# The joint round of a decoder kernel: the turn of the averaged scores goes behind the whole network product, the turn of the attention's norm into its middle

## The chip, the cores and the metric

The kernel runs on one core of a Trainium2 chip. The metric is the device time of one execution in microseconds (us). TensorE (PE) multiplies matrices and turns (transposes) tiles, VectorE (DVE), ScalarE (ACT) and GpSimd (POOL) work on elements, and SyncE (SP) starts transfers. Each engine works through its own instructions in their written order; semaphores tie the orders together.

## What is computed

The reference is a decoder of two layers over x of 16 batches x 256 rows x 256 columns, in float32. The first layer is a windowed attention, a cross attention over 77 context rows, and a network with 8 experts of which each row takes one. The second layer, which holds the change, is cut here to its core:

```python
# L1_attn: a state over the 16 batches (RWKV), then channel mixing
xx = ln(x); k, v, r = mixes of xx and of the batch before, times Wk, Wv, Wr
x = x + (sigmoid(r) * wkv(k, v)) @ Wo.T
yy = ln(x); x = x + sigmoid(rr) * (square(relu(kk)) @ Wcv.T)
# L1_xattn: attention over the context, averaged over 4 heads, steers a state space model
scores = Q @ K.T / sqrt(32)                  # 4 heads, 77 context rows
topv, topi = top_k(scores, 32); attn = softmax over those 32, zero elsewhere
attn_mean = attn.mean(heads); c_t = attn_mean @ V
scale_in, shift_in, scale_out, shift_out = c_t @ W_film_in, c_t @ W_film_out
x = layernorm(x_text) * (1 + g * scale_in) + g * shift_in
y = s4d(x)                                   # through a Fourier transform
xt = x_text + y * (1 + g * scale_out) + g * shift_out
xt = layernorm(xt + gelu(layernorm(xt) @ W1 + b1) @ W2 + b2)
# L1_ffn: product with the signs of a weight matrix, scale, bias, clip
```

## The kernel before, in words

The first layer takes up to about 815 us. The second layer is one block, `mixing_and_state_space` (from line 1430), with one written program for each engine. Its loop has 20 rounds, `for n in range(B + 4)` with B = 16 batches, and each round works on five batches at once, each at another stage: t = n (state), c = n - 1 (channel mixing, then the norm hE, queries and keys), j = n - 2 (scores, the 32 largest, average, film), i = n - 3 (Fourier transform, spectrum, inverse, network) and p = n - 4 (last norm, signs, output). A stage whose batch isn't in 0 to 15 is left out: rounds 0 to 2 have no network product, round 16 has no state batch and round 17 no hE either.

What sets the order around the change is written by hand in three places. (Line numbers are those of the kernel before.)

- TensorE, lines 2481 to 2551. A round ends with `hidden(i, 1)`, `network(n, i, 0, ...)` and the first half of `network(n, i, 1, ...)` (24 matmuls at L2462), then `turn_average` (L2399; it waits for `am`, turns its two 128x77 tiles into the bank p_T, L2403), the other half of the network product (8 matmuls, L2462), `turn_E` (L2361; turns the norm hE into the same bank p_T, four matmuls at L2287), `film(j, 0)` (L2406; waits for amT, two products of 512 columns in four matmuls at L2413), `queries_keys` (L2366; waits for hT; L2369, L2371, L2372) and `film(j, 1)`, which waits for `hs`, VectorE's use of the first film product. The next round begins with `keys_D` (L2305), `turn_2` and `values_D`.
- ScalarE, lines 2211 to 2278. After the two `gelu` come `h_E(c)` (the norm hE, L2032), `average(j)` (copies the turned average from p_T to amT, L2170), `n_2(t)` (the norm before channel mixing, L2032, which `turn_2` of the next round reads), in rounds 0 and 1 `keep_context` (copies projected context tiles from PSUM to SBUF, L2163), then `turned(e["Th"], e["hT"], c)` (copies turned hE to xT, L2142), `film(j, 0)` (L2175), `queries(c)` (L2147), `h_1(t + 2)` (L2032) and `film(j, 1)`. The next round begins with `fall_4` (L2090), the mixes of channel mixing (L2044) and others.
- VectorE, lines 1960 to 2015. `average(j)` ends with the reduction into `am` (L1867). After it come the statistics of the batch t + 2, `add_mix`, `bounded` (L1940, L1942) and `film(j, 0)` (L1873, L1875, L1877, the last of which gives `hs`). The next round brings, among others, the scores, `add_channel_mix` (L1804, which TensorE's `receptance`, L2293, waits for) and, after the inverse transform, `scale_out` (L1903).

GpSimd makes the factors of all norms (`rstd`, L1599 to L1604). No queue of transfers stands in the changed lines.

The bank p_T is used by both turns, so each must wait until ScalarE has copied what the one before left. The helper `latest(engine, (sem, i), ...)` waits for the first pair of its list whose i is a batch, `past(engine, sem, i)` for batch i of that semaphore if i is not negative:

```python
def latest(engine, *users):
    for sem, i in users:
        if 0 <= i < B:
            engine.wait_ge(sem, i + 1)
            return
```

Of the kernel before, what the change touches and what calls it, by code (L numbers as in the profile page):

```python
# [24 lines left out]
B, S, D = 16, 256, 256  # L25
# [1396 lines left out]
# [8 lines that stand above are left out]
def mixing_and_state_space(nc, args, k, place, ys_dram, cxT, cxU, out, ahead, lw, folded_film, folded_row, spectrum_in):  # L1430

    J, C, H, DH, DM = 77, 192, 4, 32, 4 * D
    FB = DM // P
# [6 lines left out]
    with ExitStack() as ctx:  # L1440
# [577 lines left out]
        def _(act):  # L2018
# [88 lines left out]
            def n_2(t):  # L2107
                act.wait_ge(d["rs2"], t + 1)
                past(act, z["T2"], t - 1)
                apply(L2, x1, n3, d["n2"])  # L2110
# [29 lines left out]
            def turned(sem, to, i):  # L2140
                act.wait_ge(sem, i + 1)
                a_.activation(xT[:], p_T[:], ACT.Copy).then_inc(to, 1)  # L2142
# [23 lines left out]
            def average(j):  # L2166
                act.wait_ge(e["amp"], j + 1)
                if j == 0:
                    act.wait_ge(d["init"], 10)
                a_.activation(amT[0:J, :], p_T[0:J, 0, :], ACT.Copy).then_inc(e["amT"], 1)  # L2170
# [40 lines left out]
            for n in range(B + 4):  # L2211
                t, c, j, i, p = n, n - 1, n - 2, n - 3, n - 4
                if t < B:
                    fall_4(t)
                if 0 <= c < B:
                    channel_mixes_A(c)
                if t < B:
                    values(t)
                    gates(t)
                    falls(t)  # L2220
                if 0 <= c < B:
                    channel_mixes_B(c)
                    gate_channel(c)
                if 0 <= p < B:
                    h_6(p)
                if 0 <= c < B:
                    rectify(c, 0, 0)
                    rectify(c, 0, 1)
                if 0 <= p < B:
                    turned(f["T6"], f["h6T"], p)  # L2230
                if t < B:
                    exps_D(t)
                if t + 1 < B:
                    n_1(t + 1)
                if n == 0:
                    keep_context(2, 3)
                if 0 <= c < B:
                    square(c, 0)
                    rectify(c, 1, 0)
                    rectify(c, 1, 1)  # L2240
                    square(c, 1)
                if t + 1 < B:
                    mixes_A(t + 1)
                    if n == 0:
                        keep_context(4, 5)
                    mixes_B(t + 1)
                if n == 1:
                    keep_context(8)
                if 0 <= i < B:
                    n_3(i)  # L2250
                if 0 <= i < B:
                    turned_3(i)
                if 0 <= j < B:
                    exps_E(j)
                    n_E(j)
                if 0 <= i < B:
                    gelu(i, 0)
                    gelu(i, 1)
                if 0 <= c < B:
                    h_E(c)  # L2260
                if 0 <= j < B:
                    average(j)
                if t < B:
                    n_2(t)
                if n == 0:
                    keep_context(6, 7)
                if n == 1:
                    keep_context(9)
                if 0 <= c < B:
                    turned(e["Th"], e["hT"], c)  # L2270
                if 0 <= j < B:
                    film(j, 0)
                if 0 <= c < B:
                    queries(c)
                if t + 2 < B:
                    h_1(t + 2)
                if 0 <= j < B:
                    film(j, 1)

        @block.tensor  # L2280
        def _(pe):
# [78 lines left out]

            def turn_E(n, j):  # L2361
                pe.wait_ge(e["h"], j + 1)
                latest(pe, (e["amT"], n - 2), (e["n3T"], n - 3), (d["mB"], n + 1))
                turn(hE[:, j % 2]).then_inc(e["Th"], 1)

            def queries_keys(j):  # L2366
                pe.wait_ge(e["hT"], j + 1)
                for kb in range(KD):
                    te.matmul(p_T[:, 0, :], Wq[:, kb, :], xT[:, kb, :], start=kb == 0, stop=kb == KD - 1)  # L2369
                rows = slice(64 * (j % 2), 64 * (j % 2) + 64)  # L2370
                te.matmul(p_T[:, 1, 0:J], Wk[:, 0, :], cxT[:, j % 2, j // 2, :], start=True, stop=False)  # L2371
                te.matmul(p_T[:, 1, 0:J], Wk[rows, 1, :], cxU[rows, j % 2, j // 2, :], start=False, stop=True).then_inc(e["qk"], 1)  # L2372
# [25 lines left out]

            def turn_average(n, j):  # L2399
                pe.wait_ge(e["am"], j + 1)  # L2400
                latest(pe, (e["n3T"], n - 3), (d["mB"], n + 1))
                for t in range(2):
                    last = te.transpose(p_T[0:J, 0, t * P:(t + 1) * P], am[:, t, :], k["ident"][:])  # L2403
                last.then_inc(e["amp"], 1)
# [51 lines left out]
            def network(n, i, a, first, end):  # L2456
                if a == 0:
                    latest(pe, (d["x1"], n), (z["g2"], n - 1), (e["Yr"], n - 3))
                for fb in range(first, end):
                    if a == 0 and fb % 2 == 0:  # L2460
                        pe.wait_ge(e[f"g{fb // 4}{fb // 2 % 2}"], i + 1)
                    last = te.matmul(p_Y[:, a, :], hid[:, fb, a * P:(a + 1) * P], W2[:, fb, :],  # L2462
                                     start=fb == 0, stop=fb == FB - 1)
                if end == FB:
                    last.then_inc(e["ffp"], 1)
# [15 lines left out]
            for n in range(B + 4):  # L2481
                t, c, j, i, p = n, n - 1, n - 2, n - 3, n - 4
                if n == 3:
                    pe.wait_ge(lw["third"], 64)
                    pe.wait_ge(cw["wide"], 16)
                if n == 4:
                    pe.wait_ge(f["sign"], 1)
                if t < B:
                    keys_D(n, t)
                if 0 <= c < B:  # L2490
                    turn_2(n, c)
                if t < B:
                    values_D(n, t)
                if 0 <= j < B:
                    scores(j)
                if t < B:
                    receptance_D(n, t)
                if n == 0:
                    context(2, 3)
                if 0 <= i < B:  # L2500
                    forward(i)
                if 0 <= c < B:
                    receptance(n, c)
                    channel(n, c, 0)
                if 0 <= p < B:
                    turn_6(n, p)
                if 0 <= c < B:
                    channel(n, c, 1)
                if 0 <= i < B:
                    inverse(n, i)  # L2510
                if t + 1 < B:
                    turn_1(n, t + 1)
                if 0 <= p < B:
                    project(n, p)
                if n == 0:
                    context(4, 5)
                if n == 1:
                    context(8)
                if 0 <= c < B:
                    channel_out(n, c, 0, 0, FB)  # L2520
                    channel_out(n, c, 1, 0, FB // 2)
                if 0 <= i < B:
                    turn_3(n, i)
                if 0 <= c < B:
                    channel_out(n, c, 1, FB // 2, FB)
                if 0 <= i < B:
                    hidden(i, 0)
                if n == 0:
                    pe.wait_ge(lw["first"], 16 * 8)
                if t < B:  # L2530
                    out_product(n, t)
                if n == 0:
                    context(6, 7)
                if n == 1:
                    context(9)
                if 0 <= i < B:
                    hidden(i, 1)
                    network(n, i, 0, 0, FB)
                    network(n, i, 1, 0, FB // 2)
                if 0 <= j < B:  # L2540
                    turn_average(n, j)
                if 0 <= i < B:
                    network(n, i, 1, FB // 2, FB)
                if 0 <= c < B:
                    turn_E(n, c)
                if 0 <= j < B:
                    film(j, 0)
                if 0 <= c < B:
                    queries_keys(c)
                if 0 <= j < B:  # L2550
                    film(j, 1)
# [78 lines left out]
```

## Time and profile before

| | us |
|---|---|
| median of 3 runs | 1811.51 |
| lowest and highest | 1810.51, 1813.48 |
| the profiled execution | 1824.46 |
| its span | 1822.8 |
| TensorE busy, share of the span | 1610.8, 88% |
| VectorE busy | 1278.0, 70% |
| ScalarE busy | 909.9, 50% |
| GpSimd busy | 649.1, 36% |

The span is the time from the first to the last instruction of the profiled execution; all rows of the trace are on its clock. Busy time of TensorE is modelled from the starts of its matmuls, which overlap by a little, so two groups one after the other may seem to share a tenth of a microsecond. "Granted clock" is the share of TensorE's full 2.4 GHz that the chip let through: 1.00, or 0.50 for 1.2 GHz. In a row of the trace, "[1.45 <-DVE E_am L1867]" says that the engine stood idle for 1.45 us before it, and that the instruction of that engine and line ended the wait.

### The profile page before, as it was taken

The page shows a single profiled execution, that of the slowest core. Times are in us where ns is not written, and L with a number is a line of the kernel's source. Part 1 is how long each engine was busy: PE and PEld are TensorE (multiplying, and loading weights), DVE is VectorE, ACT ScalarE, POOL GpSimd, SP SyncE. Part 2 cuts the span into 40 slices and gives each one's busy share as a digit, 9 for nine tenths or more (in the row PEclk, how much of TensorE's full clock was granted, in tenths as well). Part 3 has the DMA queues.
Part 4 walks back from the last instruction along what each step waited for, and adds up shares of the span by engine and source line. Part 5 has one row for each costly group of instructions (what it writes and reads, how often), then busy time and mean ns, then how long its engine had stood idle before and what let it go on. Part 6 is the DMA issues. An engine that isn't in the chain of part 4 may idle for free.

```text
span 1822.8 us, 27958 instructions
## 1 busy us (share of the span) xinstructions
PE 1610.8 (88%) x8584; PEld 1330.1 (73%) x8584; DVE 1278.0 (70%) x4255; ACT 909.9 (50%) x1943; POOL 649.1 (36%) x1005
## 2 busy tenths in 40 slices
PE   6899999997599999978869999999999999998774
PEld 3677778776489999874647777777877777786553
DVE  3566777766247666224478899999999999987751
ACT  2454444442142222226656766667776667763221
POOL 1022322222101000015435556666655655552111
PEclk9899999999699999998879999999999999999877
DMA  9992000000796565545200000000000000000000
GB/s 258 289 290 75 15 16 13 12 13 24 256 309 199 153 202 162 174 139 212 73 7 8 13 20 19 20 13 7 20 19 20 20 13 7 8 14 13 7 6 12
DMA packets 145477, 143.47 MB, mean 79 GB/s; under 512 B 22587, under 2 KB 128525, under 8 KB 145074
## 3 DMA queue, kind: packets, MB, share of 16 engines
q1 hardware_dynamic: 128321, 119.78, 21.4%
q10 hardware_dynamic: 13936, 13.50, 2.3%
q0 software_dynamic: 3072, 8.39, 1.5%
q8 instruction: 71, 1.16, 0.3%
q14 instruction: 77, 0.62, 0.1%
HBM read 87.71 MB, written 53.94 MB: 78 GB/s over the span
## 4 chain that ended last, share of the span: by engine, by line
PE 28%; DVE 21%; issue 3%; ACT 2%; POOL 1%; DMA 0%; POOLq 0%; DVEq 0%; ACTq 0%
PE E_pK L2346 6%; PE E_pK L2305 3%; PE E_pS L2413 3%; DVE E_wk L1850 3%; PE E_pY L2462 3%; DVE E_ex L1782 2%; DVE E_m L1843 2%; PE E_pY L2293 2%; PE E_pU L2422 2%; PE E_pY L2431 2%; DVE E_st L1715 1%; PE E_pY L2305 1%; PE E_pT L2287 1%; PE E_pY L2356 1%; PE E_pU L2452 1%
## 5 line engine op out<-in xcount | busy, mean ns | idle before, releaser
L1294 ACT ACTIVATE F_uT<-F_puT,F_b 128x128 f32<-128x128 f32 x312 | 88.4, 371 | 214.6 <-PE F_puT L1351 165.4
L1351 PEld LDWEIGHTS F_puT<-F_hT,F_W 128*128 128x128 f32 x1248 | 157.8, 207 | 10.3 <-DVE F_hT L1089 8.1
L1351 PE MATMUL F_puT<-F_hT,F_W 128*128 128x128 f32 x1248 | 159.6, 291 | 5.7 <-DVE F_hT L1089 5.7
L1599 POOL TENSOR_SCALAR E_var<-E_mv 128x2 f32<-128x2 f32 x80 | 44.6, 558 | 309.8 <-DVE E_mv L1719 308.2
L1364 PE MATMUL F_py<-C_W,F_uT 128*128 x624 | 141.2, 379 | 0.6 <-DVE C_shared L1101 0.6
L2452 PE MATMUL E_pU<-E_xT,E_W 128*128 128x256 f32 x512 | 122.5, 395 | 5.3 <-ACT E_hid L2193 3.1
L1364 PEld LDWEIGHTS F_py<-C_W,F_uT 128*128 128x128 f32 x624 | 115.5, 190 | 15.1 <-issue 1.0
L2356 PE MATMUL E_pY<-E_Wcv,E_hid 128*128 128x256 f32 x512 | 118.3, 385 | 8.6 <-issue 8.2
L2462 PE MATMUL E_pY<-E_W,E_hid 128*128 128x256 f32 x512 | 119.1, 387 | 0.1
L2452 PEld LDWEIGHTS E_pU<-E_xT,E_W 128*128 128x128 f32 x512 | 101.6, 199 | 21.7 <-ACT E_hid L2193 3.9
L2346 PE MATMUL E_pK<-E_cmix,E_Wck 128*128 128x256 f32 x512 | 115.9, 381 | 0.0
L2356 PEld LDWEIGHTS E_pY<-E_Wcv,E_hid 128*128 128x128 f32 x512 | 96.1, 192 | 26.5 <-issue 14.3
L1066 POOL TENSOR_SCALAR F_var<-F_mv 128x1 f32<-128x1 f32 x39 | 8.6, 222 | 290.8 <-DVE F_mv L1078 290.8
L2462 PEld LDWEIGHTS E_pY<-E_W,E_hid 128*128 128x128 f32 x512 | 98.1, 194 | 14.0 <-DVE E_x L1796 0.9
L2346 PEld LDWEIGHTS E_pK<-E_cmix,E_Wck 128*128 128x128 f32 x512 | 96.8, 191 | 12.9
L237 POOL TENSOR_SCALAR A_varB<-A_mvB 128x2 f32<-128x2 f32 x16 | 3.5, 220 | 256.2 <-DVE A_mvB L289 256.2
L1850 DVE MATCH_REPLACE8 E_wk<-E_m,E_wk 128x77 f32<-128x77 f32 x384 | 80.4, 222 | 0.0
L2193 ACT ACTIVATE E_hid<-E_pU,b 128x256 f32<-128x256 f32 x128 | 52.1, 473 | 51.2 <-PE E_pU L2452 51.0
L645 PE MATMUL A_pqa<-A_hTB,A_Wq 128*128 128x256 f32 x256 | 68.1, 413 | 2.6 <-ACT A_hTB L490 2.6
L2305 PE MATMUL E_pK<-E_mix,Wkvr 128*128 128x256 f32 x256 | 64.6, 398 | 5.0 <-DVE E_mix L1752 5.0
L1602 POOL TENSOR_TENSOR E_rs<-E_var,minus_half 128x2 f32<-128x2 f32 x80 | 62.5, 782 | 6.7
L2305 PEld LDWEIGHTS E_pK<-E_mix,Wkvr 128*128 128x128 f32 x256 | 49.9, 201 | 18.3 <-issue 12.1
(432 smaller groups left out, 4133.4 us busy)
## 6 DMA issues: line engine op xcount, KB each, us to landing
F_W<-in_L_ffn_W SPq DMA_DIRECT2D x39, 1024.0 KB, 6.0
sorted_x<-zero SPq DMA_DIRECT2D x8, 4096.0 KB, 31.6
C_W<-in_L_ffn_W ACTq DMA_DIRECT2D x8, 1024.0 KB, 7.6
F_xs<-sorted_x SPq DMA_DIRECT2D x39, 128.0 KB, 2.7
F_b<-in_L_ffn_b SPq DMA_DIRECT2D x39, 128.0 KB, 3.2
sorted_y<-C_shared ACTq DMA_DIRECT2D x39, 128.0 KB, 2.9
context_film<-E_W SPq DMA_DIRECT2D x8, 512.0 KB
out<-E_tB SPq DMA_DIRECT2D x16, 256.0 KB, 2.2
```

Of the source, the lines that this page charges most:

```text
L645: last = te.matmul(p_qa[:, half, (m % 2) * S:(m % 2 + 1) * S], Wq[:, kb, m * P:(m + 1) * P], hTB[:, kb, :], start=kb == 0, stop=kb == KD - 1)
L1294: last = nc.scalar.activation(uT[:, i % 2, f, :], p_uT[:, i % 2, half, (f % 4) * P:(f % 4 + 1) * P], ACT.Gelu, bias=b1[:, i % 2, f:f + 1])
L1351: last = nc.tensor.matmul(p_uT[:, i % 2, half, (f % 4) * P:(f % 4 + 1) * P], W1[:, i % WB, kb, f * P:(f + 1) * P], hT[:, i % 2, kb, :], st ...
L1364: last = nc.tensor.matmul(p_y[:, 0:D], uT[:, i % 2, f, :], W2[:, bass.ds(e, 1), f, :], start=f == 0, stop=f == FB - 1)
L1602: chained(g.tensor_tensor(L["rs"][:], L["var"][:], k["minus_half"][:], ALU.pow))
L1850: last = v.match_replace(wk[:, t, hd, :], m8[:, turn, t, hd, :], src[:, t, hd, :], TAKEN)
L2305: last = te.matmul(to[:, o, :], Wkvr[:, m, kb, o * P:(o + 1) * P], mix[:, m, kb, :], start=kb == 0, stop=kb == KD - 1)
L2346: last = te.matmul(p_K[:, q, :], Wck[:, kb, fb * P:(fb + 1) * P], cmix[:, 0, kb, :], start=kb == 0, stop=kb == KD - 1)
L2356: last = te.matmul(p_Y[:, a, :], hid[:, fb, a * P:(a + 1) * P], Wcv[:, fb, :], start=fb == 0, stop=fb == FB - 1)
L2413: last = te.matmul(p_S[:, q, :], amT[:, t * P:(t + 1) * P], VW[j % 2][:, q * 512:(q + 1) * 512], start=True, stop=True)
L2452: last = te.matmul(p_U[:, q, :], W1[:, kb, fb * P:(fb + 1) * P], xT[:, kb, :], start=kb == 0, stop=kb == KD - 1)
L2462: last = te.matmul(p_Y[:, a, :], hid[:, fb, a * P:(a + 1) * P], W2[:, fb, :], start=fb == 0, stop=fb == FB - 1)
```

## The change

In TensorE's order the turn of hE comes right after the first half of `network(n, i, 1, ...)`, then the other half, then the turn of the averaged scores. ScalarE's order follows: the copy of turned hE comes before the copy of the average, and `n_2` comes behind both, in rounds 0 and 1 also behind `keep_context(6, 7)` and `keep_context(9)`. The waits for the bank p_T are rewritten to fit: `turn_E` no longer waits for amT of its round, `turn_average` waits for hT, and `queries_keys` waits for amT.

```diff
@@ -2258,16 +2258,16 @@
                 if 0 <= c < B:
                     h_E(c)
-                if 0 <= j < B:
-                    average(j)
-                if t < B:
-                    n_2(t)
                 if n == 0:
                     keep_context(6, 7)
                 if n == 1:
                     keep_context(9)
                 if 0 <= c < B:
                     turned(e["Th"], e["hT"], c)
+                if 0 <= j < B:
+                    average(j)
+                if t < B:
+                    n_2(t)
                 if 0 <= j < B:
                     film(j, 0)
@@ -2360,11 +2360,12 @@
             def turn_E(n, j):
                 pe.wait_ge(e["h"], j + 1)
-                latest(pe, (e["amT"], n - 2), (e["n3T"], n - 3), (d["mB"], n + 1))
+                latest(pe, (e["n3T"], n - 3), (d["mB"], n + 1))
                 turn(hE[:, j % 2]).then_inc(e["Th"], 1)
 
             def queries_keys(j):
                 pe.wait_ge(e["hT"], j + 1)
+                past(pe, e["amT"], j - 1)
@@ -2398,7 +2399,7 @@
             def turn_average(n, j):
                 pe.wait_ge(e["am"], j + 1)
-                latest(pe, (e["n3T"], n - 3), (d["mB"], n + 1))
+                latest(pe, (e["hT"], n - 1), (e["n3T"], n - 3), (d["mB"], n + 1))
@@ -2537,12 +2538,12 @@
                     hidden(i, 1)
                     network(n, i, 0, 0, FB)
                     network(n, i, 1, 0, FB // 2)
+                if 0 <= c < B:
+                    turn_E(n, c)
+                if 0 <= i < B:
+                    network(n, i, 1, FB // 2, FB)
                 if 0 <= j < B:
                     turn_average(n, j)
-                if 0 <= i < B:
-                    network(n, i, 1, FB // 2, FB)
-                if 0 <= c < B:
-                    turn_E(n, c)
                 if 0 <= j < B:
                     film(j, 0)
```

## Rows read from the trace of the kernel before

**Rows 1.** The page: busy us, share of the span, instructions.

```profile
PE 1610.8 (88%) x8584; PEld 1330.1 (73%) x8584; DVE 1278.0 (70%) x4255; ACT 909.9 (50%) x1943; POOL 649.1 (36%) x1005
```

**Rows 2.** Stretches: length, busy of PE, PEld, DVE, ACT, POOL, granted clock, DMA.

```profile
899.50:903.00 3.50, 3.42 (x9) 2.79 (x10) 0.00 (x0) 0.36 (x2) 2.70 (x7) 0.50 0.44 122
...
1354.00:1407.00 53.00, 50.05 (x231) 41.35 (x230) 48.97 (x166) 37.33 (x79) 33.25 (x46) 1.00 0.05 17
```

**Rows 3.** The chain in order of time, round 10: start, us, what.

```profile
1379.09 1.20 DVE E_am L1867
...
1407.25 0.70 DVE E_fo L1903
...
1432.71 1.20 DVE E_am L1867
```

**Rows 4.** Timeline of TensorE, end of round 10: start, us, what, idle before.

```profile
1373.55 5.34 PE L2462 MATMUL E_pY<-E_W,E_hid 128*128 128x256 f32 x24
1380.34 0.44 PE L2403 MATMUL E_pT<-ident,E_am 128*77 128x128 f32 x2 [1.45 <-DVE E_am L1867]
1380.62 1.89 PE L2462 MATMUL E_pY<-E_W,E_hid 128*128 128x256 f32 x8
1382.35 0.60 PE L2287 MATMUL E_pT<-ident,E_hE 128*128 128x128 f32 x4
1382.79 1.88 PE L2413 MATMUL E_pS<-E_VW,E_amT 78*128 78x512 f32 x4
...
1386.04 1.98 PE L2413 MATMUL E_pS<-E_VW,E_amT 78*128 78x512 f32 x4
```

**Rows 5.** Timeline of ScalarE, the same place.

```profile
1380.82 0.38 ACT L2170 ACTIVATE E_amT<-E_pT 77x256 f32<-77x256 f32 x1 [5.26 <-PE E_pT L2403]
```

**Rows 6.** Timeline of VectorE, the same place.

```profile
1383.24 0.69 DVE L1942 TENSOR_TENSOR E_tB<-E_tB,E_X 128x512 f32<-128x512 f32 x1
1384.78 0.42 DVE L1873 TENSOR_TENSOR E_u<-E_u,E_pS 128x256 f32<-128x256 f32 x1 [0.84 <-PE E_pS L2413]
...
1385.57 0.41 DVE L1877 TENSOR_TENSOR E_hE<-E_hE,E_pS 128x256 f32<-128x256 f32 x1
```

**Rows 7.** Timeline of TensorE, rounds 2, 3 and 16.

```profile
949.00 1.08 PE L2287 MATMUL E_pT<-ident,E_hE 128*128 128x128 f32 x4 [0.56 <-ACT E_amT L2170]
...
1003.41 0.61 PE L2403 MATMUL E_pT<-ident,E_am 128*77 128x128 f32 x2 [2.68 <-DVE E_am L1867]
...
1007.54 1.88 PE L2413 MATMUL E_pS<-E_Wvf,E_amT 78*128 78x512 f32 x4
...
1702.98 0.38 PE L2403 MATMUL E_pT<-ident,E_am 128*77 128x128 f32 x2
```

**Rows 8.** Timelines of all engines, end of round 1 and start of round 2.

```profile
892.79 1.11 PE L2395 MATMUL E_pU<-E_Wvf,cxU 64*104 64x512 f32 x4
...
897.04 1.09 ACT L2032 ACTIVATE E_n<-E_x,E_nmr,E_rs 128x256 f32<-128x256 f32 x2 [3.40 <-POOL E_nmr L1604]
898.04 1.00 ACT L2163 ACTIVATE E_W<-E_pU 104x1024 f32<-104x1024 f32 x1
...
898.94 0.58 ACT L2142 ACTIVATE E_xT<-E_pT 128x512 f32<-128x512 f32 x1
...
899.58 2.08 PE L2369 MATMUL E_pT<-E_xT,E_Wq 128*128 128x256 f32 x4 [5.09 <-ACT E_xT L2142]
899.70 0.20 POOL L1604 TENSOR_TENSOR E_nmr<-E_nm,E_rs 128x2 f32<-128x2 f32 x1
...
907.10 0.91 ACT L2090 ACTIVATE E_ex<-E_diff,E_decay 128x256 f32<-128x256 f32 x2 [3.01 <-DVE E_diff L1758]
907.91 1.91 ACT L2044 ACTIVATE E_cmix<-E_pT,E_biasA,E_scaleA 128x256 f32<-128x256 f32 x4
...
911.34 1.22 DVE L1804 TENSOR_TENSOR E_cmix<-E_cmix,E_cmixB 128x1024 f32<-128x1024 f32 x1
...
912.91 1.96 PE L2293 MATMUL E_pY<-E_Wcr,E_cmix 128*128 128x256 f32 x8 [0.78 <-ACT E_gate_ L2084]
```

## The prediction, made before the change was run

> **What bounds the kernel now.** I read the page first, then the chain of waits of the last stage, then each engine's timeline for one round, then the rounds at both ends. TensorE is busy 88% and VectorE 70% of the span [rows 1]: neither alone is full. From about 893 us on, 20 rounds n = 0 to 19 run; a regular one takes 53.62 us (the chain's two reductions into `am`, 1379.09 and 1432.71 [rows 3]). The reader should see a loop of two engines there. From 1380.34 to 1407.25 the chain is all TensorE, ending in the inverse transform; from 1407.25 to the end of the reduction into `am` at 1433.9 it is all VectorE [rows 3], with no gap that another engine ends. The two meet at the turn of the averaged scores: TensorE stands 1.45 us there for `am` and only then does half a network product (1.73 us, 1380.62 to 1382.35) and the turn of hE (0.44), neither of which needs `am`; then the film product starts at 1382.79 [rows 4]. So 1.73 + 0.44 us of free work stand behind the wait. That is what the change moves.
>
> **Part 1: regular rounds, n = 4 to 14, eleven of them.** TensorE ends the first part of the network product at 1378.89 (1373.55 + 5.34), the next could start 0.16 earlier, as matmuls overlap by that much (1380.62 + 1.89 against 1382.35) [rows 4]. In the new order: turn of hE 1378.73 to 1379.17, second half to 1380.90, then the turn of the scores. `am` is there at 1380.29 (1379.09 + 1.20 [rows 3]), so TensorE no longer waits and VectorE has some 0.6 us in hand. The price is new: the copy of the turned scores to amT, hidden before by the half product, is now bare between turn and film. The turn takes 0.38 when nothing held it (row 1702.98 [rows 7]) and the copy 0.38 [rows 5]. The wait around that same copy is seen in round 2, 0.56 us at half clock (row 949.00 [rows 7]); it can't be under 0.38; I take 0.47, as the hand-overs there are partly slowed by the low clock. Film then starts at 1380.90 + 0.38 + 0.47 = 1381.75, 1.04 earlier than 1382.79. It is now started by a wait: its loads are not ahead, and the second film product, started like that, lasts 1.98 against 1.88 [rows 4], so 0.94 is left at its end. VectorE ends its own work at 1383.93 [rows 6], so its film step can begin at about 1383.87 instead of 1384.78, 0.91 earlier; the second film product starts 0.06 after that step's last instruction ends (1385.98 and 1386.04 [rows 4, 6]), so it is bound by it. I take **0.90 a round, 9.9 for eleven**; ends 0.4 (a second wait eats half) and 1.04.
> The ScalarE moves cost nothing here: the copy of turned hE runs at 1379.4 to 1380.0, beside the half product (it is 0.6 long by the equal copy in row 898.94 [rows 8]); the channel mixing's norm (n_2) slips behind amT, but its own turn on TensorE comes only behind film, queries, the second film product and the keys. Without that cover n_2 would hold film's ScalarE copy by its 1.09. The turn of hE needs ScalarE's norm of it, which stands ahead of all the moved work in ScalarE's order and is done while TensorE is in the first part of the network product. `queries_keys` gains a wait for an older amT, long fulfilled since film has waited for the newer one. No DMA moves; SP and POOL are passed by nothing.
>
> **Part 2: rounds 3 and 15.** Here the wait for `am` is 2.68 us, and the half product after it ran at half clock: 4.13 us from turn to film (1003.41 to 1007.54) where a regular round has 2.45 [rows 4, 7]. Moved ahead, 2.17 us of work fill the wait to 0.5, and film starts 0.44 + 0.47 after the turn: 4.13 - 0.91 = **3.2 each, 6.4**; round 15 repeats the pattern. Low end 2.5 each.
>
> **Part 3: round 2.** There is no network; the turn of hE stood between amT and film (949.00, 0.88 long up to film [rows 7]). It now runs in the idle time before. Gain 0.9 if the clock rises as much earlier, 0.46 if it rises at the same moment; **0.7**.
>
> **Part 4: rounds 16 and 17.** TensorE comes late and does not wait (row 1702.98 has no idle time [rows 7]). Nothing is filled, and the bare copy is paid, with the film's 0.10 and overlap: about 0.65 each, **-1.3**; ends -0.9 and -1.5.
>
> **Part 5: the start, rounds 0 and 1, where ScalarE's order matters.** In round 1 ScalarE stood until 897.04 for the factor of n_2, and behind n_2 were the copy of a context tile (1.00) and of turned hE (0.58), so the query product began only at 899.58, after 5.09 us of idle, at a granted clock of 0.50, 1.2 GHz [rows 2, 8]. In the new order these two run first: the context product ends at 893.90 (892.79 + 1.11), the copies at 893.94 to 895.45, queries from 895.5, 4.1 us earlier. The idle time before is then 1.0, less than the 1.45 that leaves the clock at 1.00 [rows 2, 4], so I expect queries and keys at 2.4 GHz, half as long. The next bound is then POOL: it ends the norm of the next batch at 899.90 (row 899.70 [rows 8]), ScalarE applies it (1.09) and begins the falls at 901.05 instead of 907.10; 0.81 + 1.81 of ScalarE and 1.22 of VectorE later, with hand-overs, 905.05, the receptance product starts, against 912.91 [rows 8]: **7.9**. Low end 4.0, if the clock falls all the same. In round 0 n_2 goes behind two context copies, the second of which can't start until its product ends: a loss between nothing and its own 1.09 [rows 8]; **-0.35**, since most of the wait for that product is used by the first copy.
>
> **Sum.** 9.9 + 6.4 + 0.7 - 1.3 + 7.9 - 0.35 = 23.2 us. The profiled execution took 1824.46 (span 1822.8), so 1801.2 (span 1799.6); the runs' median 1811.51 is 12.95 below it, and the same 23.2 comes off: **1788.3**. By the ends of all parts: gains of 0.4 x 11 + 5.0 + 0.46 - 1.5 + 4.0 - 1.09 = 11.3 to 1.04 x 11 + 6.4 + 0.9 - 0.9 + 7.9 = 25.7, so 1785.8 to 1800.2.
>
> **The clock, and a rule against the change.** Each regular round has a few idle spots on TensorE, the longest of 1.45 us, and its granted clock stays 1.00 [rows 2, 4]; the change replaces the longest by one of 0.47. The Trainium skill, in "TensorE: Matmul & The Clock Gate", section "HAM oscillation", warns that frequent small idle spots between groups of matmuls can make the clock fall again and again. By that rule a new spot before film in every round could cost; by this trace it would not, and the sum keeps to the trace.
>
> **Rivals.**
> 1. *Round 1 gives only its earlier start* (the clock falls anyway, or another wait follows): 4.0 for 7.9, total 19.3, 1792.2. For it: a long quiet stretch stands around it. Chance 0.15.
> 2. *A second wait in regular rounds*: the film step of VectorE comes 0.1 to 0.5 later than I have it, or `am` comes after TensorE again. Gain 0.4 a round: total 17.7, 1793.8. For it: VectorE's 0.84 of idle before film shrinks to nothing [rows 6], so both engines are now tight. Chance 0.17.
> 3. *The loop is VectorE's alone*, so regular rounds gain nothing: 13.3, 1798.2. Against: the chain runs 26.9 us on TensorE in each round [rows 3]. It is also what we should see if the moved order changed nothing there. Chance 0.05.
> 4. *Slower: the bare wait drops the clock at film.* If film and queries ran at 1.2 GHz in rounds 3 to 16, film would be 1.7 longer (it doubles) and the query product 1.0 (half of round 1's 2.08 at a clock of 0.50 [rows 2, 8]): 2.7 x 14 = 38 on top of 1788.3, so 1826. It decides from 1.65 us a round on. Against it: the longer spots of now leave the clock at 1.00. Chance 0.03.
> The forecast has 0.57; another mix of parts that ends within 0.2% of before 0.03.
>
> **How the numbers follow.** 0.2% (3.6 us) is about what a measurement of this kernel can tell from no change. The forecast and rivals 1 to 3 are all faster by more: 0.94; same 0.03; slower 0.03. The range takes the forecast's ends and rivals 1, 2 and 3, with 1 to 1.5 us on either side for the spread of the runs shown (1810.51 to 1813.48): 1784 to 1801.
>
> **What would show it.** Right: regular rounds of 52.7 us; at the turn of the scores no idle time on TensorE and then 0.4 to 0.6 "<-ACT E_amT" before film; the wait of 2.68 gone and the network product in rounds 3 and 15 at full clock; queries of round 1 at 895.5 and at 2.4 GHz, the receptance product of round 2 near 905; in rounds 16 and 17 film 0.6 later after the network. Wrong: a turn that still waits for `am`, a query product at half clock in round 1, or TensorE waiting for VectorE's film step for more than 0.2.

## The result, and the profile after

In the same series the changed kernel takes 1792.47 us in the median of four runs (1791.12 to 1799.51), the kernel before 1812.49 (four runs, 1810.51 to 1817.97): a ratio of 0.9884, 95% interval 0.9845 to 0.9923. Two later series with the same code gave 0.9859 (0.983 to 0.9889) and 0.9869 (0.9827 to 0.9911). The forecast of 1788.3 against 1811.51 is a ratio of 0.9872. So the kernel is faster, by about as much as was said: 20.0, 22.9 and 21.0 us between medians, where 23.2 had been summed. The measured 1792.47 lies inside the stated range of 1784 to 1801.

The profiled execution after has a span of 1797.8, 25.0 less than before. Not all of this is the change. The rounds begin at another moment in every execution: `add_mix` of round 0 (L1752), which the change leaves alone, starts at 859.17 before and at 856.32 after, and between 842.5 and 859.2 in all profiles of this study. So below, next to medians, stands **the rest**: the span less the start of that instruction. It is 963.63 before and 941.48 after, 22.15 less, and tells a few microseconds apart where medians can't.

The page after, busy time of each engine (answers to [rows 1]; the work is the same, so TensorE's share is higher by the time it no longer stands):

```profile
PE 1606.7 (89%) x8584; PEld 1323.5 (74%) x8584; DVE 1278.7 (71%) x4255; ACT 909.8 (51%) x1943; POOL 651.2 (36%) x1005
```

Stretches after: the query and key products of round 1, the film, query and key products of round 2, and one regular round (columns as in [rows 2]):

```profile
892.80:896.30 3.50, 3.46 (x17) 2.94 (x18) 0.61 (x3) 1.42 (x3) 3.10 (x7) 1.00 0.44 122
936.90:950.50 13.60, 13.56 (x26) 7.94 (x27) 5.79 (x12) 3.16 (x7) 5.95 (x10) 0.51 0.15 42
1327.00:1380.00 53.00, 51.03 (x237) 42.30 (x236) 49.60 (x167) 38.23 (x80) 33.31 (x46) 1.00 0.05 17
```

A regular round is at a granted clock of 1.00 as before, and so are now the products of round 1 [rows 2 had 0.50]. Those of round 2 are at half clock.

The chain of waits after, up to the turn of the scores and film of round 11, a regular round like the round 10 of [rows 3] (all rows of 1396 to 1422 below are of round 11):

```profile
1396.66 0.98 ACT E_n L2032 x2
...
1408.71 5.18 PE E_pY L2463 x24
1413.89 0.44 PE E_pT L2287 x4
1414.33 1.73 PE E_pY L2463 x8
1416.06 0.23 PE E_pT L2404 x2
...
1416.31 0.39 ACT E_amT L2170
...
1416.74 1.98 PE E_pS L2414 x4
```

VectorE's 26.7 us from the inverse transform to `am`, which stood in the chain before, are gone from it: the chain now reaches film through TensorE and, earlier in the round, ScalarE. The same place of round 11 in TensorE's timeline (to be read beside [rows 4]):

```profile
1408.55 5.34 PE L2463 MATMUL E_pY<-E_W,E_hid 128*128 128x256 f32 x24
1413.73 0.60 PE L2287 MATMUL E_pT<-ident,E_hE 128*128 128x128 f32 x4
1414.16 1.89 PE L2463 MATMUL E_pY<-E_W,E_hid 128*128 128x256 f32 x8
1415.89 0.38 PE L2404 MATMUL E_pT<-ident,E_am 128*77 128x128 f32 x2
1416.74 1.98 PE L2414 MATMUL E_pS<-E_Wvf,E_amT 78*128 78x512 f32 x4 [0.47 <-ACT E_amT L2170]
...
1420.14 1.98 PE L2414 MATMUL E_pS<-E_Wvf,E_amT 78*128 78x512 f32 x4
```

ScalarE there (answers to [rows 5]):

```profile
1416.31 0.38 ACT L2170 ACTIVATE E_amT<-E_pT 77x256 f32<-77x256 f32 x1 [1.35 <-PE E_pT L2404]
```

VectorE there (answers to [rows 6]):

```profile
1414.12 1.20 DVE L1867 TENSOR_REDUCE E_am<-E_ex 128x154 f32<-128x616 f32 x1
...
1418.27 0.69 DVE L1942 TENSOR_TENSOR E_tB<-E_tB,E_X 128x512 f32<-128x512 f32 x1
1418.88 0.41 DVE L1873 TENSOR_TENSOR E_u<-E_u,E_pS 128x256 f32<-128x256 f32 x1
...
1419.67 0.41 DVE L1877 TENSOR_TENSOR E_hE<-E_hE,E_pS 128x256 f32<-128x256 f32 x1
```

Read the three together. The turn of the scores has no idle time before it: `am` ended at 1415.32 (1414.12 + 1.20), 0.57 earlier. Film waits 0.47 for ScalarE's copy, no more. VectorE's first film instruction follows L1942 without a gap, where 0.84 stood before, and its last ends at 1420.08, 0.06 before the second film product. Every one of these was forecast, and successive turns of the scores lie 52.70 apart (52.7 forecast).

TensorE in rounds 2, 3 and 16 (answers to [rows 7]):

```profile
926.96 1.11 PE L2287 MATMUL E_pT<-ident,E_hE 128*128 128x128 f32 x4 [2.56 <-ACT E_hE L2032]
935.76 0.71 PE L2404 MATMUL E_pT<-ident,E_am 128*77 128x128 f32 x2 [7.69 <-DVE E_am L1867]
936.94 3.78 PE L2414 MATMUL E_pS<-E_VW,E_amT 78*128 78x512 f32 x4 [0.47 <-ACT E_amT L2170]
...
943.34 3.78 PE L2414 MATMUL E_pS<-E_VW,E_amT 78*128 78x512 f32 x4
946.91 3.58 PE L2305 MATMUL E_pK<-E_mix,Wkvr 128*128 128x256 f32 x8
...
994.23 0.44 PE L2404 MATMUL E_pT<-ident,E_am 128*77 128x128 f32 x2 [0.51 <-DVE E_am L1867]
995.14 1.98 PE L2414 MATMUL E_pS<-E_Wvf,E_amT 78*128 78x512 f32 x4 [0.47 <-ACT E_amT L2170]
...
1679.73 0.38 PE L2404 MATMUL E_pT<-ident,E_am 128*77 128x128 f32 x2
1680.59 1.98 PE L2414 MATMUL E_pS<-E_VW,E_amT 78*128 78x512 f32 x4 [0.47 <-ACT E_amT L2170]
```

Round 3's wait is 0.51 for 2.68, round 16 pays the bare copy, and in round 2 both film products and the keys run at half clock.

All engines, end of round 1 and start of round 2 (answers to [rows 8]):

```profile
891.28 1.02 ACT L2163 ACTIVATE E_W<-E_pU 104x1024 f32<-104x1024 f32 x1 [0.30 <-PE E_pU L2396]
892.20 0.59 ACT L2142 ACTIVATE E_xT<-E_pT 128x512 f32<-128x512 f32 x1
892.85 1.13 PE L2370 MATMUL E_pT<-E_xT,E_Wq 128*128 128x256 f32 x4 [1.02 <-ACT E_xT L2142]
...
897.50 1.09 ACT L2032 ACTIVATE E_hD<-E_X,E_nmr,E_rs 128x256 f32<-128x256 f32 x2 [1.69 <-POOL E_nmr L1604]
898.50 0.89 ACT L2090 ACTIVATE E_ex<-E_diff,E_decay 128x256 f32<-128x256 f32 x2
...
901.30 1.22 DVE L1804 TENSOR_TENSOR E_cmix<-E_cmix,E_cmixB 128x1024 f32<-128x1024 f32 x1 [0.41 <-issue]
```

The copies no longer stand behind the norm that waits for POOL; the queries begin after 1.02 of idle instead of 5.09 and take 1.13 instead of 2.08; the next bound is POOL's `nmr`, as forecast.

### The profile page after: what moved, and what is told of

Its sections match the earlier page's. It is cut to its first block, busy times and chain, and to the rows that moved or that the text cites. A ratio compares the mean times of both kernels' runs of the same rounds, so it can differ in the third digit from the quotient of the medians.

```text
span 1797.8 us, 27973 instructions
## 1 busy us (share of the span) xinstructions
PE 1606.7 (89%) x8584; PEld 1323.5 (74%) x8584; DVE 1278.7 (71%) x4255; ACT 909.8 (51%) x1943; POOL 651.2 (36%) x1005
## 4 chain that ended last, share of the span: by engine, by line
PE 34%; ACT 10%; DVE 6%; issue 3%; POOL 1%; DMA 0%; ACTq 0%; POOLq 0%; DVEq 0%
PE E_pU L2453 6%; PE E_pY L2463 5%; PE E_pS L2414 3%; PE E_pK L2346 3%; PE E_pK L2305 3%; PE E_pY L2293 3%; PE E_pY L2356 2%; ACT E_mix L2044 2%; ACT E_mixB L2044 2%; PE E_pU L2423 2%; PE E_pY L2305 1%; PE E_pT L2287 1%; ACT E_ex L2105 1%; ACT E_hid L2119 1%; PE E_pS L2382 1%
## 5 line engine op out<-in xcount | busy, mean ns | idle before, releaser
L1351 PEld LDWEIGHTS F_puT<-F_hT,F_W 128*128 128x128 f32 x1248 | 150.2, 198 | 11.1 <-DVE F_hT L1089 9.0
L1351 PE MATMUL F_puT<-F_hT,F_W 128*128 128x128 f32 x1248 | 152.0, 282 | 6.6 <-DVE F_hT L1089 6.6
L2356 PE MATMUL E_pY<-E_Wcv,E_hid 128*128 128x256 f32 x512 | 116.6, 381 | 8.6 <-issue 8.2
L2356 PEld LDWEIGHTS E_pY<-E_Wcv,E_hid 128*128 128x128 f32 x512 | 94.9, 190 | 26.0 <-issue 14.3
L645 PEld LDWEIGHTS A_pqa<-A_hTB,A_Wq 128*128 128x128 f32 x256 | 53.6, 216 | 14.9 <-ACT A_hTB L490 6.9
```

The lines of the kernel that those rows point to most:

```text
L645: last = te.matmul(p_qa[:, half, (m % 2) * S:(m % 2 + 1) * S], Wq[:, kb, m * P:(m + 1) * P], hTB[:, kb, :], start=kb == 0, stop=kb == KD - 1)
L1351: last = nc.tensor.matmul(p_uT[:, i % 2, half, (f % 4) * P:(f % 4 + 1) * P], W1[:, i % WB, kb, f * P:(f + 1) * P], hT[:, i % 2, kb, :], st ...
```

## The experiments

Each kernel was timed beside the kernel before. "The change" is the changed kernel; times are medians, ratios are against the kernel before. The rest is compared between profiles with the same length of `channel_out` (L2356) in round 2, for a reason told under the fourth experiment.

**The change again.** No edit.

> The changed kernel once more, as the base for the others of this set. The sum of the prediction with the parts as its first profile has them gives 22 us less than before; the runs so far say 20. Theory (all parts real): 20 to 23 less than the kernel before. Rival (part of the 25 us between the two profiles is other work): the profile again shows a time ahead of round 0 that differs by some us from before, which no part of the change touches. In round 2 the granted clock stayed at half until 950 us in the first profile; if that belongs to the change, the film product there again lasts 3.8 and the keys product behind it 3.6.

1790.37, ratio 0.9859 (0.983 to 0.9889); rest 941.69 against 941.48 in the first profile; regular rounds 52.70. The regular part of the trace repeats.

**ScalarE's order at the start, alone.** The kernel before, with only this:

```diff
-                if t < B:
+                if 1 < n < B:
                     n_2(t)
...
                     turned(e["Th"], e["hT"], c)
+                if n < 2:
+                    n_2(t)
```

> The kernel before with ScalarE's new order in rounds 0 and 1 alone: n_2 behind the context copies and behind the copy of turned hE. Theory (part 5 is 7.9 less 0.35, independent of the rest): 7.5 us less than before, about 1805; queries of round 1 start some 4 us earlier and run at 2.4 GHz; regular rounds stay at 53.6. Rival 1 (only the earlier start counts): 4 less. Second rival (the start gains only together with TensorE's order): 0.

1805.66, ratio 0.9954 (0.9929 to 0.998): 7.6 less. The queries of round 1 start after 1.02 of idle and take 1.13, and the receptance product of round 2 starts 46.24 after `add_mix` where it was 53.74 before: 7.5 less, as expected. Regular rounds keep 53.63. The rest, 960.05, is only 3.6 less than before, because the clock stayed low for longer behind the turn of the scores in round 2 (see Part 3 in the last sections). One norm, moved on one engine in two rounds of twenty, carries a third of the gain.

**The change without it.** `n_2` in its old place in rounds 0 and 1, all else as changed.

> The changed kernel with n_2 back in its old place in rounds 0 and 1 alone. Theory: the rest of the change remains, 9.9 + 6.4 - 1.3 and what round 2 gives or takes (+0.7 to -2): 13 to 15.5 us less than before, 7.5 more than the change; regular rounds at 52.7. Rival (the parts share one gain): less than 4 more than the change.

1798.40, ratio 0.991 (0.9879 to 0.9941): 8.0 more than the change; by the rest 948.12 against 941.69, 6.4 more. The query product stands 5.10 idle and is at half clock again. The receptance product of round 2 starts 52.35 after `add_mix`, 6.1 later than in the change and not 7.5, since the clock came back within the key product of round 1 (3.25 long, 3.78 in the profile of before). So the size of Part 5 hangs in part on when the clock comes back. The parts add: 7.6 and 14.9 less, each alone, make 22.5, and the whole change in the same series was 22.9 less.

**The old order in round 2.** The change, but in round 2 TensorE turns hE behind the scores, and ScalarE copies in that order:

```diff
-                if 0 <= c < B:
+                if 0 <= c < B and n != 2:
                     turn_E(n, c)
...
                     turn_average(n, j)
+                if n == 2:
+                    turn_E(n, c)
```

> The changed kernel with the old order in round 2 alone: turn of the scores, its copy, then turn and copy of hE. Theory A (the early turn of hE, standing alone in TensorE's idle time, has to do with the clock coming back late): film and keys of round 2 run at 2.4 GHz sooner, 2 to 3 us less than the change. Theory B (when the clock comes back is chance, not the order): the order costs the turn's own 0.9 at half clock, so 0.5 to 1 more than the change, and the rise of the clock lies anywhere in both.

1793.10, ratio 0.9873 (0.9843 to 0.9904); rest 944.31. TensorE's timeline in its round 2:

```profile
904.98 8.83 PE L2358 MATMUL E_pY<-E_Wcv,E_hid 128*128 128x256 f32 x32 [2.46 <-issue]
...
928.01 0.71 PE L2406 MATMUL E_pT<-ident,E_am 128*77 128x128 f32 x2 [11.35 <-DVE E_am L1867]
929.27 1.09 PE L2289 MATMUL E_pT<-ident,E_hE 128*128 128x128 f32 x4 [0.56 <-ACT E_amT L2170]
930.15 3.62 PE L2416 MATMUL E_pS<-E_VW,E_amT 78*128 78x512 f32 x4
...
936.39 3.78 PE L2416 MATMUL E_pS<-E_VW,E_amT 78*128 78x512 f32 x4
```

Two lines need care. The long channel product takes 8.83 here and 7.14 in the change's first two profiles, after the same 2.46 of idle: in some executions the clock falls there and in some not. The third profile of the change, below, has 8.83, so this is chance and no effect of an order; it is worth 1.7. Like with like (both 8.83), film starts 83.26 after `add_mix` in the old order and 82.31 in the new (929.77 - 847.46): the moved turn is worth 0.95 at that place. And the second film product is 3.78 long here too, in the old order. So the new order is not what keeps the clock low in round 2.

**Only the turn of the scores moved.** The kernel before, with the scores turned behind the whole network product and hE still behind them:

```diff
-                if 0 <= j < B:
-                    turn_average(n, j)
                 if 0 <= i < B:
                     network(n, i, 1, FB // 2, FB)
+                if 0 <= j < B:
+                    turn_average(n, j)
                 if 0 <= c < B:
                     turn_E(n, c)
```

> The kernel before with one thing moved on TensorE: the turn of the scores goes behind the whole network product, the turn of hE stays behind it (and waits for amT, as before). ScalarE's order is the old one. Theory: the second half product alone (1.73 us) covers the 1.45 us wait; the copy to amT is bare all the same, now between the two turns, and film starts as early as with the full change: regular rounds 52.7, rounds 3 and 15 some 2.5 us each, 16 and 17 half a microsecond lost each: 13 to 15 less than before. Rival (the norm's turn in the middle is what pays): regular rounds above 53.2, under 8 less.

1800.38, ratio 0.9924 (0.9896 to 0.9952); rest 950.44, 13.2 less than before; regular rounds 52.69. This one move has the whole regular gain. TensorE's waits in it, from 1200 to 1500 (engine and line that waited, for whom: us in total, times, longest):

```profile
PE E_pT L2287 <- ACT E_amT L2170: 3.4, 6, 0.6
```

The turn of hE waits 0.6 a round for the bank. TensorE ends later than in the change there, and the period is the same: the wait costs nothing, since VectorE's film step is the later one (its first instruction, at 1265.39, follows L1942 without a gap there too).

**Only the turn of hE moved.** The change, but with the scores turned right behind hE, ahead of the second half of the network product.

> The changed kernel with the turn of the scores back in the middle of the network product: the norm's turn first, then the turn of the scores, then the second half. ScalarE's order is the new one, with the start of rounds 0 and 1. Theory: only the turn of hE (0.44) fills the wait for am, the copy to amT is covered again: regular rounds 53.15, TensorE still waits about 1 us for am, and rounds 3 and 15 keep a wait of 2.2 and a half product at 1.2 GHz. In all 7.5 (start) + 5 (0.44 in eleven rounds) + 1 to 2: 13 to 15 less than before, 6 to 8 more than the change. Rival: the bare copy costs more than it seems, and this is as fast as the change.

1799.45, ratio 0.9917 (0.9888 to 0.9946); regular rounds 53.19.

```profile
PE E_pT L2404 <- DVE E_am L1867: 6.2, 6, 1.0
```

TensorE still waits 1.0 a round for `am` (1.45 before): the 0.44 of the turn of hE fills its part of the wait and no more. So in regular rounds one move alone gives 0.93 and the other 0.43, and together 0.92: they overlap.

**The bare copy hidden again.** The change, with the scores turned after three quarters of the product, the last quarter over the copy:

```diff
-                    network(n, i, 1, FB // 2, FB)
+                    network(n, i, 1, FB // 2, 3 * FB // 4)
                 if 0 <= j < B:
                     turn_average(n, j)
+                if 0 <= i < B:
+                    network(n, i, 1, 3 * FB // 4, FB)
```

> The changed kernel with the turn of the scores after three quarters of the second column half of the network product, the last four matmuls (0.87 us) behind it, where they cover the copy to amT. Theory (VectorE's film step is the bound once TensorE is this early: it follows its own work without idle time): film starts 0.2 to 0.3 earlier but the second film product does not, regular rounds stay at 52.7, rounds 16 and 17 win 0.6 each, 3 and 15 lose 0.3: within 2 us of the change. Rival (TensorE is the bound, the 0.47 can be had): regular rounds at 52.3 to 52.4, 4 to 5 less than the change.

1796.09, ratio 0.9872 (0.9842 to 0.9903); rest 943.57; regular rounds 52.70, no change. The 0.47 before film is gone (the turn waits 0.2 for `am` instead), and a new wait stands one step later:

```profile
PE E_pS L2414 <- DVE E_hE L1877: 1.9, 6, 0.3
```

TensorE reaches the second film product 0.3 early and waits for VectorE. So the film step of VectorE bounds this place, as Part 1 had it: film alone starting earlier moves nothing. At the film of round 17 this kernel is 1.5 ahead of the third profile of the change, as expected of rounds 16 and 17, but it loses 1.4 behind it (see the end of Part 3), so its rest shows only 0.2.

**The bare copy hidden and VectorE's order eased.** In addition, `bounded(p)` behind `film(j, 0)` on VectorE:

```diff
-                if 0 <= p < B:
-                    bounded(p)
                 if 0 <= j < B:
                     film(j, 0)
+                if 0 <= p < B:
+                    bounded(p)
```

> The same, and on VectorE the clip and last sum of the output (bounded, 1.1 us) go behind the film step, ahead of keys. Theory: the bound named for the run before is gone; film's step starts 0.1 after its product and regular rounds take 52.3 to 52.4: 4 us less than the change. Rival (VectorE is late at the next place: keys, then the scores and the sum that the receptance product waits for): regular rounds at 52.7 or more, with idle time of TensorE now ahead of the receptance product.

1789.64, ratio 0.9866 (0.9836 to 0.9895); regular rounds 52.51. VectorE now waits for film again:

```profile
1250.18 0.42 DVE L1873 TENSOR_TENSOR E_u<-E_u,E_pS 128x256 f32<-128x256 f32 x1 [0.60 <-PE E_pS L2414]
```

The step it bounded is eased, but only 0.19 a round comes of it, half of what I expected; `am` is 0.2 late (0.9 in five rounds), as in the split alone (1.1 in six). The rest is 940.18 against 943.74 of the change with the same `channel_out`.

**Round 2 with TensorE kept at work.** The forecast for round 2 had been off, by the clock. Here are 16 matmuls whose result is not used, put in its idle time:

```diff
+                if n == 2:
+                    for q in range(16):
+                        te.matmul(p_U[:, 0, :], Wkvr[:, 0, 0, 0:P], Wkvr[:, 0, 1, :], start=q == 0, stop=q == 15)
                 if 0 <= j < B:
                     turn_average(n, j)
```

> The change, with 16 extra matmuls of 256 columns in round 2, in the idle time of TensorE ahead of the turn of the averaged scores (7.69 us of it in the change's profile); their result is not used. At half clock they take 0.43 each, 6.9 us, so they end before the scores are averaged. Theory: what I mis-sized in round 2 is the clock, and it is low there because TensorE stands idle; kept at work, it is granted the full clock earlier, and the first film product of round 2 is about 2.0 long instead of 3.78, the query product 1.0 instead of 1.9, the key products of the next round 3.6 less for both; everything behind comes 5 to 7 us earlier (about 1784 in the median, a film product at 927 of full clock). Rival: the low clock lasts its 14.6 us whatever TensorE does, counted from the turn of hE then: film still at 0.50, no gain, 0 to 2 us. Second rival: the extra matmuls at half clock run past the end of the reduction and the turn of the scores comes later: 0 to 3 us slower than the change.

1786.40, ratio 0.9847 (0.9799 to 0.9894). TensorE in its round 2:

```profile
920.97 0.66 PE L2287 MATMUL E_pT<-ident,E_hE 128*128 128x128 f32 x4 [2.56 <-ACT E_hE L2032]
921.46 7.07 PE L2547 MATMUL E_pU<-Wkvr 128*128 128x256 f32 x32
929.77 0.44 PE L2404 MATMUL E_pT<-ident,E_am 128*77 128x128 f32 x2 [1.24 <-DVE E_am L1867]
930.68 1.98 PE L2414 MATMUL E_pS<-E_VW,E_amT 78*128 78x512 f32 x4 [0.47 <-ACT E_amT L2170]
...
934.03 1.99 PE L2414 MATMUL E_pS<-E_VW,E_amT 78*128 78x512 f32 x4
935.85 1.89 PE L2305 MATMUL E_pK<-E_mix,Wkvr 128*128 128x256 f32 x8
```

The turn of the scores comes as before, 8.80 after that of hE, but film is 1.98 for 3.78, its second product and the keys likewise, and the next turn of the scores follows after 51.73 instead of 58.74: 7.0 for round 2, at the upper end of the theory. The rest is 934.56 against 941.69 (both with 7.14), 7.1 less.

Where the clock fell has to be read with care. In the profile after it is at 0.50 from 926.5 on, in the idle time of 2.56 ahead of the turn of hE, and until 950.2: so it fell ahead of the 7.69, not in it. In the kernel with 16 it never fell, from 906 to 945, though the same 2.56 stood there.

(A matmul of 256 columns is two instructions here: it takes 0.44 at full clock, not 0.22 as I reckoned, so the filler fitted only because it ran at full clock.)

**The same with 28.**

> The same with 28 extra matmuls: 12.1 us at half clock, 6.0 us at full. If the clock rises within the first few us of them, they end before the reduction into the averages and the gain is that of 16 or a little more (no new idle time before film); if it stays at half throughout, they end some 3.5 us after the averages are there, and the kernel is 3 us slower than the change in round 2 if film is still at half clock, or 2 to 4 us faster if film then runs at full.

1792.44, ratio 0.9878 (0.9837 to 0.9919).

```profile
915.31 13.94 PE L2547 MATMUL E_pU<-Wkvr 128*128 128x256 f32 x56
929.08 0.38 PE L2404 MATMUL E_pT<-ident,E_am 128*77 128x128 f32 x2
```

With twice the length per matmul that I had reckoned, it runs past `am`: the turn of the scores comes 14.27 after that of hE instead of 8.80. 5.5 of the 7 are given back. (The rest, 940.00, is 3.7 less than the third profile's 943.74; 1.6 of it is round 2, the other 2.1 lies in later rounds and isn't explained. The medians, 1792.44 and 1791.44, show no gain.) Here the clock fell as the filler began, and came back while it ran. Stretches of this kernel, then of the third profile of the change (columns as in [rows 2]):

```profile
914.60:918.00 3.40, 3.19 (x11) 2.66 (x12) 3.30 (x20) 0.76 (x2) 1.78 (x5) 0.63 0.01 2
918.00:922.00 4.00, 4.00 (x18) 3.43 (x18) 3.83 (x18) 0.00 (x0) 1.41 (x2) 0.89 0.00 0
...
919.70:921.00 1.30, 1.11 (x4) 0.71 (x4) 1.26 (x4) 0.10 (x2) 0.49 (x1) 0.54 0.03 6
...
933.00:940.00 7.00, 7.00 (x14) 3.95 (x13) 3.22 (x8) 1.82 (x5) 3.00 (x4) 0.50 0.13 37
```

So work on unused products at half clock was followed by the full clock within the filler, and idle time was not: what the filler buys is that film meets a clock that never fell or has come back. Why film, queries and keys, which kept TensorE busy too, ran at half clock for about 14 us before it came back stays open.

**All together.** The change with the split, the later `bounded`, the 16 matmuls, and in round 0 `n_2` in its old place.

> The change with the pieces that each had something for them: the turn of the scores after three quarters of the network product and the signs' bounds behind VectorE's first film step (0.19 a round in its own run, so 2), in round 0 the norm before channel mixing in its old place on ScalarE (0.2), and 16 extra matmuls in round 2. If they add, 2 + 0.2 + 5 to 7 = 7 to 9 us less than the change, about 1782; if the extra matmuls give nothing, 2 us less, 1788 to 1789.

1778.42 (1777.28 to 1788.16), ratio 0.981 (0.9767 to 0.9853). Rest 933.01, 10.7 less than the change's 943.74 (both with 8.83); regular rounds 52.51, round 2 51.67. It is the fastest of all kernels here; 7.0 of the 10.7 is round 2's clock and 2.1 the eleven regular rounds. Here too the clock fell as the filler began (0.56 from 915 to 918) and came back in it (0.87 to 921, then 1.00). Against the change beside it, 13 between medians, but the two intervals overlap, so by timing alone it is likely and not certain.

**The change a third time**, beside these three.

> The changed kernel as it is, beside the three others on the same chip: 0.986 to 0.989 of the time before.

1791.44, ratio 0.9869 (0.9827 to 0.9911); rest 943.74, with `channel_out` of 8.83: 2.05 more than the second profile, 1.7 of it from that one product.

## Why the prediction was right, step by step

The shifts between the two profiles, from one place to the next (each is how much earlier the after profile reaches it than the one before):

| step | forecast | profile |
|---|---|---|
| ahead of round 0 | 0 | 2.85 |
| Part 5, round 0 | -0.35 | -0.20 |
| Part 5, round 1 (receptance at 902.58 for 912.91) | 7.9 | 7.68 |
| Part 3, round 2 (turn of the scores of round 3) | 0.7 | -1.15 |
| Part 2, round 3 (turn to film) | 3.2 | 3.22 |
| Part 1, eleven regular rounds | 9.9 | 9.98 |
| Part 2, round 15 | 3.2 | 3.07 |
| Part 4, rounds 16 and 17 | -1.3 | -1.32 |
| behind round 17 | 0 | 0.87 |
| sum | 23.2 | 25.0 |

**Part 1** was right in size and in its cause. The wait for `am` went, the bare copy came at 0.47, and of the 1.04 won at film's start 0.90 was left, because VectorE's own work ends there. The split kernel confirms the bound: an earlier film alone moves nothing. Rival 3 is refuted too: VectorE alone did not set the loop before the change, since the move gives 0.9. Rival 2's second wait did not show.

**Parts 2 and 4** held within 0.15 us each: the half product and the turn fill the wait of 2.68 down to 0.51, and where there was no wait the bare copy costs 0.64 to 0.68.

**Part 5** held: ScalarE's order had made two ready copies stand behind a norm whose factor was 3.40 late, and 4.1 of the 7.7 is the earlier start of the queries; the other 3.6 comes with query and key products at full clock and the waits behind them. Rival 1 needed the clock to fall at the queries all the same; it stayed at 1.00.

**Part 3 is the step that was off**, by 1.85, and by the clock, not by the order. I took the profile of before as typical, where the second film product is already at full clock (955.97, 1.98 long). In every other profile without the filler, ten of them, four with the turn of hE in the old place or the start in the old order, it is 3.78. From the turn of the scores in round 2 to the receptance product of the next round it is 18.44 before, 22.22 in the old-order kernel and 21.22 in the profile after (21.30 and 21.49 in the two other profiles of the change): the reorder gives 0.7 to 1.0 by these (at the least 0.4 against the 21.89 below), near what was said, and the longer stretch at half clock costs 3.8 (22.22 - 18.44). The fall of the clock in `channel_out` that the before profile had, and the after profile had not, gives 1.65 back (34.83 before and 33.18 after from the receptance product to the turn of the scores). 1.0 - 3.8 + 1.65 is the -1.15 measured. The last is chance, since one program shows both. The longer stretch is not the change's doing either: the kernel with only the turn of the scores moved has the order of before on every engine up to the end of round 2, where there is no network product, and its second film product there is 3.78 long (947.74), its way from the turn to the receptance product 21.89. The kernel with ScalarE's start alone, with TensorE's order of before, has 3.77 and 22.04. So the 1.98 and the 18.44 of the profile of before were its luck, one profile of eleven without the filler, and the step that failed is to have taken them as the rule. Set right for it, the profiles fit the sum well: at equal `channel_out` (8.83) the rest goes from 963.63 to 943.74, 19.89 less, and with the 3.45 that the before profile was lucky by (21.89 - 18.44) an estimate of the usual gain is 23.3. A gain between medians need not show either. The 2.85 ahead of round 0 is no work of the change either. The 0.87 behind round 17 is the clock too, as far as the profiles tell: from the film of round 17 to the end it is 68.66 to 69.25 in the four profiles whose second film product there is long (3.25 to 3.59; 3.29 before), and 67.22 to 67.90 in the ten where it is 1.98 (as after). The four are the kernels that still turn the scores ahead of part of the network product, but two others that do so have 1.98, so whether the order matters there is not shown.

**Rival 4** (the new spot drops the clock at film) is refuted: turns of the scores lie 52.70 to 52.72 apart through the regular rounds, and the stretch of one of them has 1.00. The warning that TensorE idles briefly between groups of matmuls so often that the clock swings stands in the Trainium skill, "TensorE: Matmul & The Clock Gate", in the section "A second HAM failure mode: psum-queue depth-cycling", right behind the section "HAM oscillation" that the prediction names. It did not bite here: a spot of 0.47 per round in place of one of 1.45 leaves the clock alone, by this trace.

**What bounds it now.** I read it so that two legs, TensorE's with ScalarE and VectorE's, end nearly together in a regular round: the chain no longer names VectorE though its film step has no gap, and easing that step gives only 0.19. No run sets the next bound apart, so this is a reading and not shown.

## What to carry to other kernels

When an engine waits in its written order and ready work stands behind the wait, put that work ahead of it, and then price the hand-over that the work had hidden: here 2.17 us of work moved, 1.45 of wait went, 0.47 came bare, and 0.90 was left because the other engine had 0.84 of slack. Read the slack of that other engine from the same place before summing. And check each engine's order at the ends of a pipeline too: two copies behind one late norm, in a single round, cost 7.7 us, and a low clock that lasted through an idle time into a few long products cost 7.

## What the runs showed of the hardware that I had not expected

- Kept at work through its idle time of 7.69 in round 2, TensorE ran what followed at 2.4 GHz, in all three kernels with the filler, also in the two where the clock fell as the filler began. Idle, it ran the next 14.4 us at 1.2 GHz (935.76 to 950.2 in the profile after), though it had work all that time but for 0.47. Unused matmuls bought 7.0 us.
- The same idle time of 2.46 (2.45 in the profile of before) ahead of `channel_out` in round 2 was followed by a fall of the clock in ten profiles (8.83) and by none in four (7.14). The same program shows both. A single profile can't tell what such a spot costs.
- The half clock behind the turn of the scores in round 2 lasted 8 us in one profile (before) and 14.4 to 15.7 in the ten others without the filler, one of which has the same order on every engine up to there.
- A hand-over from TensorE through ScalarE and back took 0.85 in all: 0.38 of turn, then 0.47, of which the copy is 0.38.
